# A four-layer graph network on one core: one-hots by VectorE, edge steps and the tail in another order

## The chip, the cores and the metric

The kernel runs on one core of one Trainium2 chip. The metric is the device time of one execution in microseconds. The kernel before takes 243.12 us in the median of three runs (242.83 to 243.68).

## The reference, cut to what matters

128 nodes with 512 features, 4096 edges sorted by target, four layers one after the other, each followed by a residual and a layer norm (LN). Everything is float32.

```
L0: q, k, v = x@Wq+bq, x@Wk+bk, x@Wv+bv            # 8 heads of 64
    scores masked by the adjacency, softmax over n, attn @ v, @ Wo + bo
    h1  = LN(x + attn_out)*g1 + be1                 # "LN1"
    out = LN(h1 + relu(h1@W1+b1)@W2 + b2)*g2 + be2  # "LN2"
x  = LN(x + out)
L1: h = mish([x[src], x[dst], edge_attr] @ W1 + b1) # 4096 edges
    m = mish(h @ W2 + b2);  agg = segment_sum(m, dst)
    u = mish([x, agg] @ W3 + b3);  y = x + u@W4 + b4
    out = LN(y)*gamma + beta
x  = LN(x + out)
L2: two graph convolutions, out = Ahat@relu(Ahat@(x@W1)+b1)@W2 + b2
x  = LN(x + out)
L3: h = x@Ws^T + (Cn@x)@Wn^T + bias;  out = LN(h)*gamma + beta
x  = LN(x + out)
```

x[src] @ W1a is computed as a matmul of A = x@W1a (128 nodes) with a one-hot matrix ST (node by edge) that picks the source of each edge; DT does the same for the targets. The edge_attr part of the product, 64 features deep, is computed ahead of time and kept in C.

## The kernel before, in words

Each engine has its own instruction list, in an order written out by hand, with semaphores between them; nothing is reordered at run time. The names:

- **Edge groups.** The 4096 edges are eight groups of 512, and four pairs of groups. ST and DT hold eight stretches of 512 columns, one for each group, in float32r. C holds 8 x 4 tiles of 128x512 (four blocks of 128 hidden features).
- **One-hots of the targets** (L523 to L530, and `onehot_out`, L319): TensorE turns Dbf, the bfloat16 one-hot with edges on the partitions, by 32 matmuls against an identity, in eight PSUM fillings over four banks. ScalarE copies each into DT (eight copies of 128x512, L321). This lies behind the product with Wo and ahead of the transposes of LN1's output.
- **One-hots of the sources** (`source_onehots`, L1015): the ids, spread by DMA to all partitions as two 1 MB pieces `ids0` and `ids1`, are compared with the partition's number by VectorE, eight instructions of 128x512, four ahead of the graph matrices (L1023) and four behind them.
- **Edge steps** (`edge_term`, L538). A step makes two C tiles: six matmuls (three terms, two groups) into two banks, which ScalarE reads with the bias added (`edge_term_out`, L323). Steps 0 to 11 (the ring) go over banks 5, 6, 7, 0 in turn; steps 12 to 15 over banks 1 to 4, around and behind the products A and B. A bank must have been read before it is filled again. Steps 0 to 2 lie between the four parts of the first feed-forward product (F1), steps 3 to 6 in the second (F2), steps 7 to 10 in the wait for LN2, step 11 behind the transposes of LN2's output xs (L661 to L665).
- **LN2 on VectorE.** `residual` (L888) takes each half of F2's result as it is signalled (f2_done), adds xw, takes statistics; then norm with gain, a second norm, xs. TensorE transposes xs into banks 3 and 4; VectorE makes xhi, xlo and xT, and TensorE computes A and B ("AB", L668 to L673).
- **Edge loop** (L753 on). For g = 0..7: `second_layer(g)` is 48 matmuls of 512 columns (h and W2, each split in a high and a low part), `first_layer(g+1)` 16, `sum_messages(g-1)` 8. VectorE and ScalarE work beside it: z1_out, z2_out, mish, low parts.
- **Tail.** update (W3), o = u@W4 (banks 2 and 4), residual with xw, norm with gain, y; the transposes of y; z = y@G1; r0; Ahat@r0; r1g; p1g; `p1g@G2` added to xw in banks 5 and 6; statistics; xs; the last layer in banks 4 and 0; last norms; output. GpSimd computes each 1/sqrt(var) (`inverse_root`, L284, tile rstd). WsR and WnR are transposed on the way (`turn`, eight of four transposes; ScalarE's `turned_out`, L434) and split in high (`ws_high`, L429) and low parts (`weight_low`, L1093).
- **SyncE's DMA list**, in order: inputs and weights up to W1raw; a wait for the last target one-hot and for the edge counts (L240, L241), F2; a wait for Wo's product, ids0, ids1; three rows of LN2; W2raw; a wait for xs, seven late rows, L1_b2; G1, G2; W3, W4, WsR, WnR each behind a group of the loop.

A source one-hot and a step of the ring:

```
v.tensor_scalar(ST_by_tile[:, q, h], row_ids[h][:, q], iota_col[:, 0:1], None, ALU.is_equal)
for i, (w, x) in enumerate([(Wchi, EAThi), (Wclo, EAThi), (Wchi, EATlo)]):
    for o in range(2):
        done = mm(banks[o][:, :], w[part, P * j:P * (j + 1)], x[part, q, :], start=i == 0, stop=i == 2)
```

Of the kernel before, what the change touches and what calls it, by code (L numbers as in the profile page):

```python
# [40 lines left out]
def gnn_kernel(nc, a, out):  # L41

    ctx = ExitStack()
    with ctx:
# [69 lines left out]
        thin = overlay(("bvo", 87, 2, F32), ("bvo_parts", 89, 2, F32R))  # L114
        ctx.enter_context(nc.sbuf_tensor("region", [P, 95 * D], F32))
# [19 lines left out]
        ST_by_tile = ST.rearrange("p (q o i s e) -> p q s i o e", q=PAIRS, o=2, i=GT, s=2)  # L135
# [22 lines left out]
        PRE = (bank[5], bank[6], bank[7], bank[0])  # L158
        EA_BANKS = (bank[4], bank[4], bank[3], bank[3])
        F1_BANKS = bank[1:5]  # L160
        DT_BANKS = (bank[7], bank[1], bank[2], bank[0])
# [20 lines left out]
        DT_UNIT, C_UNIT = 0, G  # L182
        RING_STEPS = KC * (PAIRS - 1)
        UNITS = C_UNIT + 2 * RING_STEPS
        TURNED_FIRST = 5
        LATE_BANKS = ((bank[3], bank[4]), (bank[1], bank[2]))

        S = {}
        for name in ("x_in warm_ready ids_in row_ids_in0 row_ids_in1 st_ready vecs_in ea_in wq_in0 wq_in1 wq_in2 wq_in3 wk_in0 wk_in1 wk_in2 wk_in3 ids_twice wv_in wo_in f1_in f2_in w1_in wc_in w2_in w3_in w4_in g_in ws_in wn_in b1g_in "
# [32 lines left out]
        def _(sp):  # L222
# [17 lines left out]
            sp.wait_ge(S["pre_done"], C_UNIT)  # L240
# [5 lines left out]
            for name in EARLY_ROWS[2:]:  # L246
                load_row(name)
            sp.dma_start(W2raw, w_view(a["L1_gnn_W2"])).then_inc(S["w2_in"], 16)


            sp.wait_ge(S["nx_ready"], 4)
            for name in LATE_ROWS:
                load_row(name)
            sp.wait_ge(S["pre_done"], C_UNIT + 2 * KC)
            load_row("L1_gnn_b2")
            sp.wait_ge(S["ab_done"], 2)
            sp.dma_start(G1, w_view(a["L2_gnn_W1"])).then_inc(S["g_in"], 16)
            sp.dma_start(G2, a["L2_gnn_W2"]).then_inc(S["g_in"], 16)
# [7 lines left out]
            sp.dma_start(WnR, w_view(a["L3_gnn_W_neigh"])).then_inc(S["wn_in"], 16)  # L266
            sp.wait_ge(S["y_final0"], 1)
# [24 lines left out]
        def _(act):  # L292
# [20 lines left out]
            for j in range(KC):  # L313
                bias_out(qT[:, j, :], quarter(bank[2], j), "L0_gnn_bq", j).then_inc(S["qk_ready"], 1)
            for j in range(KC):
# [3 lines left out]
            def onehot_out(dst, unit, g):  # L319
                act.wait_ge(S["pre_done"], unit + g + 1)  # L320
                act.activation(dst[:, GE * g:GE * (g + 1)], DT_BANKS[g % 4][:, :], ACT.Copy).then_inc(S["pre_read"], 1)  # L321

            def edge_term_out(steps):  # L323

                for s in steps:
                    q, j = s // KC, s % KC
                    for o in range(2):
                        k = 2 * s + o
                        if s < RING_STEPS:
                            act.wait_ge(S["pre_done"], C_UNIT + k + 1)  # L330
                            src, signal = PRE[(C_UNIT + k) % 4], "pre_read"
                        else:
                            act.wait_ge(S["late_done"], k - 2 * RING_STEPS + 1)
                            src, signal = LATE_BANKS[s % 2][o], "late_read"
                        bias_out(C[:, 2 * q + o, j, :], src[:, :], "L1_gnn_b1", j).then_inc(S[signal], 1)
# [24 lines left out]
            act.wait_ge(S["wc_in"], 32)  # L360
            act.activation(Wchi, Wc, ACT.Copy).then_inc(S["wc_hi"], 1)
            features_high(0)
            for g in range(G):
                onehot_out(DT, DT_UNIT, g)
            features_high(1)
            features_high(2)
            act.wait_ge(S["ao_done"], 1)
            act.wait_ge(S["wo_done"], 2)
            act.wait_ge(S["w1_in"], 16)
            for i in range(4):  # L370
                relu_out(i)
                w1_high(i)
                if i >= 1:
                    edge_term_out(range(i - 1, i))
            features_high(3)
            edge_term_out(range(3, RING_STEPS))
            act.wait_ge(S["w2_in"], 16)
            act.wait_ge(S["st_ready"], 2 * PAIRS)
# [59 lines left out]
            turned_out(range(TURNED_FIRST))  # L438
            for h in range(2):
                act.wait_ge(S["y2T_done"], h + 1)  # L440
                act.activation(half(flat(xT[:, :, :]), h), (bank[2], bank[4])[h][:, 0:D // 2], ACT.Copy).then_inc(S["y2T_ready"], 1)
            ws_high(0)
            ws_high(1)
            turned_out(range(TURNED_FIRST, 2 * KC))
            act.wait_ge(S["g1_done"], 1)
            act.activation(r1g, bank[3][:, 0:HID2], ACT.Relu).then_inc(S["g1_ready"], 1)
            ws_high(2)
            act.wait_ge(S["g2_done"], 1)
            act.activation(p1g, bank[4][:, 0:N], ACT.Copy).then_inc(S["g2_ready"], 1)
            ws_high(3)  # L450
# [19 lines left out]
        def _(pe):  # L470
# [44 lines left out]
            def free_bank(n):  # L515
                if n >= 4:
                    pe.wait_ge(S["pre_read"], n - 3)
                return PRE[n % 4]

            def turn_onehots(by_edge, groups):  # L520

                for g in groups:
                    b = DT_BANKS[g % 4]  # L523
                    if g >= 4:
                        pe.wait_ge(S["pre_read"], g - 3)
                    for i in range(GT):
                        done = mm(quarter(b, i), by_edge[:, tile_of(g, i), :], ident_bf[:, :], start=True, stop=True)
                    done.then_inc(S["pre_done"], 1)

# [7 lines left out]
            def edge_term(steps):  # L537

                for s in steps:
# [3 lines left out]
                    if s < RING_STEPS:  # L543
                        banks, signal = [free_bank(C_UNIT + 2 * s + o) for o in range(2)], "pre_done"
                    else:
                        if s >= RING_STEPS + 2:
                            pe.wait_ge(S["late_read"], 2 * (s - RING_STEPS - 1))
                        banks, signal = LATE_BANKS[s % 2], "late_done"
# [74 lines left out]
            pe.wait_ge(S["ident_bf_ready"], 1)  # L623
            pe.wait_ge(S["cols_ready"], 1)
            turn_onehots(Dbf, range(G))
            pe.wait_ge(S["ea_lo"], 1)
            turn_features(1)
            transpose_halves(O_BANKS, y, S["nx_ready"], 0, S["nT_done"])
            turn_features(2)
            pe.wait_ge(S["nT_ready"], 2)  # L630
            pe.wait_ge(S["f1_in"], 16)
            for i in range(4):
                if i < 2:
                    pe.wait_ge(S["pre_read"], 6 + i)
# [3 lines left out]
                if i == 1:  # L638
                    pe.wait_ge(S["wc_lo"], 1)
                if i >= 1:  # L640
                    edge_term(range(i - 1, i))
# [37 lines left out]
            def first_layer(g, js=range(KC), ks=range(len(terms))):  # L679

                for j in js:
# [3 lines left out]
                    elif ks[0] == 0:  # L685
                        pe.wait_ge(S["pre_read"], UNITS - 3 + u)
# [43 lines left out]
            pe.wait_ge(S["st_ready"], 2 * PAIRS)  # L730
# [46 lines left out]
            o_banks = (bank[2], bank[4])  # L777
            pe.wait_ge(S["u_hi"], 2)
            for b in range(2):
                columns_by(o_banks, uThi, W4hi, b, (0, 1), 0, None)  # L780
# [32 lines left out]
            pe.wait_ge(S["b1g_in"], 16)  # L813
            mm(bank[3][:, 0:HID2], ident[:, :], b1g[:, :], start=True, stop=False)
            pe.wait_ge(S["r0_ready"], 1)
            mm(bank[3][:, 0:HID2], Ahat[:, :], r0, start=False, stop=True).then_inc(S["g1_done"], 1)
            pe.wait_ge(S["wt_ready"], 2 * KC)
            pe.wait_ge(S["g1_ready"], 1)
            mm(bank[4][:, 0:N], r1g, Ahat[:, :], start=True, stop=True).then_inc(S["g2_done"], 1)
            for h in range(2):  # L820
                pe.wait_ge(S["xw_ready"], 1 + h)
                mm((bank[5], bank[6])[h][:, 0:D // 2], ident[:, :], half(xw, h), start=True, stop=False)
# [3 lines left out]

            pe.wait_ge(row_in["L3_gnn_bias"], 16)
# [35 lines left out]
        def _(dve):  # L863
# [24 lines left out]
            def residual(banks, extra, signal):  # L888

                for h in range(2):  # L890
                    dve.wait_ge(signal, h + 1)
# [77 lines left out]

            dve.wait_ge(S["scores_done"], 1)  # L970
# [22 lines left out]
            dve.wait_ge(S["wc_hi"], 1)  # L993
            v.tensor_tensor(Wclo, Wc, Wchi.bitcast(F32), ALU.subtract).then_inc(S["wc_lo"], 1)
# [20 lines left out]
            def source_onehots(h):  # L1015

                dve.wait_ge(S[f"row_ids_in{h}"], 16)
                for q in range(PAIRS):
                    v.tensor_scalar(ST_by_tile[:, q, h], row_ids[h][:, q], iota_col[:, 0:1], None, ALU.is_equal).then_inc(S["st_ready"], 1)

            source_onehots(0)
# [3 lines left out]
            source_onehots(1)  # L1025
# [5 lines left out]
            st = residual((bank[1], bank[2]), xw, S["f2_done"])  # L1031
# [8 lines left out]
            out_halves(xT_flat, xs_banks, S["nT_done"], 2, S["nT_ready"])  # L1040
            def w2_low(cs):
# [4 lines left out]
            dve.wait_ge(S["ab_done"], 1)  # L1046
            v.tensor_copy(Ahi, bank[1][:, :]).then_inc(S["ab_ready"], 1)
# [46 lines left out]

            for j in range(KC):
# [9 lines left out]
            for g in range(G):  # L1105
# [22 lines left out]
                z2_out(g, 3)  # L1128
                if g >= G - 2:
# [85 lines left out]
```

## Time and profile before

| | us |
|---|---|
| median of three runs | 243.12 (242.83 to 243.68) |
| the profiled execution | 242.47 |
| its span in the profile | 240.7 |
| PE (TensorE matmul) busy | 228.5 |
| DVE (VectorE) busy | 162.7 |
| ACT (ScalarE) busy | 130.1 |
| POOL (GpSimd) busy | 5.9 |

All times below are microseconds from the start of the span, except where a duration is meant. The span is 1.8 us less than the profiled execution's own time, and that execution is 0.65 us under the median. "PE" is TensorE, "L552" is a line of the kernel; a line can be that of a helper. The chain of waits is the work that ended last, followed back from the end.

### The profile page before, as it was taken

The numbers are of one execution on the slowest core, as the hardware profiler recorded it, in microseconds if no ns is written. First come the engines' busy times: TensorE is split into PE (matmuls) and PEld (weight loads), VectorE is DVE, ScalarE is ACT, GpSimd is POOL, SyncE is SP. The second block draws the span as 40 slices with busy tenths as digits, with TensorE's granted clock in tenths as the row PEclk, the third lists the DMA queues.
The fourth block names the chain that finished last, engine by engine and source line by source line (L and its number), as shares of the span: only waits on it lengthen the run. The fifth ranks groups of instructions, "written<-read, shape, count | busy, mean of one in ns | idle before, by whom it ended". The sixth has DMA issues, their size and how long they took to land.

```text
span 240.7 us, 3320 instructions
## 1 busy us (share of the span) xinstructions
PE 228.5 (95%) x1255; PEld 184.3 (77%) x1255; DVE 162.7 (68%) x291; ACT 130.1 (54%) x240; POOL 5.9 (2%) x17
## 2 busy tenths in 40 slices
PE   8999999997999999999999999999999999998980
PEld 4958788664766887888888888888888888997670
DVE  3956846687679655865856847758568556567695
ACT  0635289748549835745635646557475533159500
POOL 1000100001000000000000000000000000000101
PEclk9999999999999999999999999999999999999996
DMA  6999979910680000009031040040000000000001
GB/s 228 309 407 404 389 235 408 342 54 0 190 242 7 0 0 0 3 18 326 5 106 72 0 176 0 3 174 0 0 0 3 0 0 0 3 0 1 3 0 44
DMA packets 12039, 24.97 MB, mean 104 GB/s; under 512 B 988, under 2 KB 1908, under 8 KB 11640
## 3 DMA queue, kind: packets, MB, share of 16 engines
q1 hardware_dynamic: 11232, 24.25, 28.2%
q10 hardware_dynamic: 792, 0.51, 0.8%
q8 instruction: 10, 0.16, 0.3%
q14 instruction: 5, 0.04, 0.1%
HBM read 24.50 MB, written 0.26 MB: 103 GB/s over the span
## 4 chain that ended last, share of the span: by engine, by line
PE 89%; DVE 4%; ACT 3%; issue 2%; POOL 1%; POOLq 0%; DVEq 0%; ACTq 0%
PE bank L706 36%; PE bank L689 13%; PE bank L495 8%; PE bank L504 6%; PE bank L552 4%; PE bank L569 3%; PE bank L716 3%; PE bank L717 3%; PE bank L593 2%; PE bank L513 1%; PE bank L484 1%; ACT DT L321 1%; ACT WsT L434 1%; PE bank L668 1%; POOL rstd L284 1%
## 5 line engine op out<-in xcount | busy, mean ns | idle before, releaser
L706 PE MATMUL bank<-W2hi,Hhi 128*128 128x512 f32 x128 | 49.8, 389 | 0.0
L706 PE MATMUL bank<-W2hi,Clo 128*128 128x512 f32 x128 | 49.8, 389 | 0.0
L706 PE MATMUL bank<-W2lo,Hhi 128*128 128x512 f32 x128 | 49.8, 389 | 0.0
L394 ACT ACTIVATE Mhi<-M 128x512 fp32r<-128x512 f32 x32 | 20.2, 632 | 44.4 <-DVE M L1075 44.4
L1080 DVE TENSOR_TENSOR Mlo<-M,Mhi 128x512 fp32r<-128x512 f32 x32 | 22.1, 690 | 22.0 <-ACT M L395 22.0
L1075 DVE TENSOR_TENSOR M<-bank,b2r 128x512 f32<-128x512 f32 x32 | 22.0, 688 | 12.6 <-PE bank L717 7.6
L706 PEld LDWEIGHTS bank<-W2hi,Clo 128*128 128x128 f32 x128 | 24.0, 188 | 5.0
L706 PEld LDWEIGHTS bank<-W2lo,Hhi 128*128 128x128 f32 x128 | 24.0, 188 | 5.0
L706 PEld LDWEIGHTS bank<-W2hi,Hhi 128*128 128x128 f32 x128 | 24.0, 188 | 5.0
L387 ACT ACTIVATE Hhi<-C 128x512 fp32r<-128x512 f32 x32 | 20.0, 624 | 11.4 <-DVE C L1061 11.1
L305 ACT ACTIVATE C<-bank,cols 128x512 f32<-128x512 f32 x32 | 19.9, 686 | 10.5 <-PE bank L552 10.5
L1061 DVE TENSOR_TENSOR C<-bank,C 128x512 f32<-128x512 f32 x32 | 21.4, 689 | 5.1 <-PE bank L689 4.1
L1066 DVE TENSOR_TENSOR Clo<-C,Hhi 128x512 fp32r<-128x512 f32 x32 | 22.0, 688 | 3.7 <-ACT C L388 3.6
L689 PE MATMUL bank<-ST,AB 128*128 128x512 f32 x64 | 20.0, 399 | 0.0
L388 ACT ACTIVATE C<-C 128x512 f32<-128x512 f32 x32 | 19.7, 617 | 0.0
L395 ACT ACTIVATE M<-M 128x512 f32<-128x512 f32 x32 | 19.7, 616 | 0.0
L689 PE MATMUL bank<-DT,AB 128*128 128x512 f32 x64 | 19.4, 390 | 0.0
L689 PEld LDWEIGHTS bank<-ST,AB 128*128 128x128 f32 x64 | 11.6, 188 | 3.9 <-DVE C L1061 1.0
L689 PEld LDWEIGHTS bank<-DT,AB 128*128 128x128 f32 x64 | 12.0, 188 | 2.6
L716 PE MATMUL bank<-Mhi,Dg 128*128 128x512 f32 x32 | 12.6, 395 | 0.0
L717 PE MATMUL bank<-Mlo,Dg 128*128 128x512 f32 x32 | 12.5, 389 | 0.0
L284 POOL TENSOR_TENSOR rstd<-mv,mhalf 128x1 f32<-128x1 f32 x8 | 4.7, 588 | 206.1 <-DVE mv L915 193.8
(227 smaller groups left out, 332.7 us busy)
## 6 DMA issues: line engine op xcount, KB each, us to landing
F<-in_L_gnn_W SPq DMA_DIRECT2D x2, 2048.0 KB, 14.1
W1raw<-in_L_gnn_W SPq DMA_DIRECT2D x1, 2048.0 KB, 22.7
ids<-in_src SPq DMA_DIRECT2D x2, 1024.0 KB, 13.0
W<-in_L_gnn_W SPq DMA_DIRECT2D x1, 2048.0 KB, 9.2
Wq<-in_L_gnn_Wq SPq DMA_DIRECT2D x4, 256.0 KB, 3.7
Wk<-in_L_gnn_Wk SPq DMA_DIRECT2D x4, 256.0 KB, 5.6
Wv<-in_L_gnn_Wv SPq DMA_DIRECT2D x1, 1024.0 KB, 9.2
ea<-in_edge_attr SPq DMA_DIRECT2D x1, 1024.0 KB, 11.2
```

Of the source, the lines that this page charges most:

```text
L305: return act.activation(dst, src, func, bias=cols[:, col[name] + j:col[name] + j + 1])
L387: act.activation(Hhi[:, g % 2, j, :], C[:, g, j, :], ACT.Mish)
L388: act.activation(C[:, g, j, :], C[:, g, j, :], ACT.Mish).then_inc(S["h_hi"], 1)
L394: act.activation(Mhi[:, t, :], M[:, t, :], ACT.Mish)
L689: done = mm(ST1[u % 3][:, :], w[:, P * j:P * (j + 1)], x[:, GE * g:GE * (g + 1)], start=k == 0, stop=k == len(terms) - 1)
L706: done = mm(ST2[t][:, :], x[:, c, e], w[:, c, :], start=c == 0 and i == 0, stop=c == KC - 1 and i == 2)
L716: mm(AGG[:, :], Dg[:, t, :], Mhi[:, t, :], start=g == 0 and t == 0, stop=False)
L717: done = mm(AGG[:, :], Dg[:, t, :], Mlo[:, t, :], start=False, stop=g == G - 1 and t == GT - 1)
L1061: v.tensor_tensor(C[:, g, j, :], ST1[u % 3][:, :], C[:, g, j, :], ALU.add).then_inc(S["z1_read"], 1)
L1066: v.tensor_tensor(Hlo[:, g, j, :], C[:, g, j, :], Hhi[:, g % 2, j, :].bitcast(F32), ALU.subtract).then_inc(S["h_lo"], 1)
L1075: v.tensor_tensor(M[:, t, :], ST2[t][:, :], row["L1_gnn_b2"], ALU.add).then_inc(S["z2_read"], 1)
L1080: v.tensor_tensor(Mlo[:, t, :], M[:, t, :], Mhi[:, t, :].bitcast(F32), ALU.subtract).then_inc(S["m_lo"], 1)
```

## The change

- **Target one-hots** are no longer turned by TensorE or copied by ScalarE; VectorE makes them as it makes those of the sources. For pairs 0 and 1 (groups 0 to 3) both kinds are made ahead of the loop, in four instructions each of 128x512: sources for both halves ahead of the graph matrices; targets of half 0 inside LN2's residual, between its two halves; targets of half 1 behind the copy into xT. For groups 4 to 7 each group takes one instruction of 512 and two of 256 columns, in the loop at g = 1 to 4, behind z2_out(g, 2) and z2_out(g, 3).
- **DMAs.** The target ids are loaded twice, 1 MB for each half: into ids0 and ids1 as soon as the source one-hots have read these, then into two pieces for the loop; the source ids once more for the loop (2 MB). W2raw is now queued behind the first target ids, and the wait for the target one-hots ahead of F2 is gone. Late rows, G1 and G2 are loaded at the end of the loop instead of behind LN2.
- **Edge steps.** Steps 0, 1, 2 go where the target one-hots were turned, step 3 behind the third part of F1, steps 4 and 5 into F2, steps 6 to 10 behind F2 (five in LN2), step 11 as before. Step 1 uses banks 1 and 2, step 8 banks 3 and 4, the others (5, 6) or (7, 0): three pairs in LN2. The transposes of xs wait until step 8 has been read.
- **Wchi and Wclo** are made earlier (ScalarE between the biases of q and k, VectorE ahead of the softmax).
- **Tail.** Half 1 of the residual xw is put into bank 4 by a matmul with the identity ahead of u@W4, so VectorE takes half 1's statistics from the bank. The row L2_b2 is put into banks 5 and 6 by TensorE ahead of time; xw is then (y - mean) * rstd alone, and r0 is finished before it. Low parts of WsT are moved away from in front of r0 and from beside GpSimd's root (`weight_low` 0, 1 and 2). ScalarE copies four turned blocks, not five, ahead of the transposed y.

```diff
-            sp.wait_ge(S["pre_done"], C_UNIT)
             sp.wait_ge(S["ct_done"], 1)
             sp.dma_start(F2, w_view(a["L0_gnn_W2"])).then_inc(S["f2_in"], 16)
...
+            for h in range(2):
+                sp.wait_ge(S["st_ready"], 2 * (h + 1))
+                sp.dma_start(other[f"ids{h}"], by_partition(a["dst"][E // 2 * h:E // 2 * (h + 1)], E // 2)).then_inc(S[f"dst_ids_in{h}"], 16)
             sp.dma_start(W2raw, w_view(a["L1_gnn_W2"])).then_inc(S["w2_in"], 16)
...
-            turn_onehots(Dbf, range(G))
-            pe.wait_ge(S["ea_lo"], 1)
+            edge_term(range(0, 1))
             turn_features(1)
+            edge_term(range(1, 2))
+            turn_features(2)
             transpose_halves(O_BANKS, y, S["nx_ready"], 0, S["nT_done"])
-            turn_features(2)
+            edge_term(range(2, 3))
...
-                if i == 1:
-                    pe.wait_ge(S["wc_lo"], 1)
-                if i >= 1:
-                    edge_term(range(i - 1, i))
+                if i == 2:
+                    edge_term(range(3, 4))
...
                 columns_by((bank[1], bank[2]), ffT, F2, h, range(0, 3), 0, FC - 1)
-                edge_term(range(2 * h + 3, 2 * h + 4))
+                edge_term(range(h + 4, h + 5))
                 columns_by((bank[1], bank[2]), ffT, F2, h, range(3, FC - 2), 0, FC - 1)
-                edge_term(range(2 * h + 4, 2 * h + 5))
...
-            edge_term(range(7, RING_STEPS - 1))
+            edge_term(range(6, 8))
             pe.wait_ge(S["graph_ready"], 2)
+            pe.wait_ge(S["ea_lo"], PAIRS)
+            edge_term(range(8, RING_STEPS - 1))
+            pe.wait_ge(S["pre_read"], 18)
             transpose_halves((bank[3], bank[4]), xs, S["nx_ready"], 2, S["nT_done"])
...
+            for h in range(2):
+                first_onehots(ST_by_tile, "row_ids_in", h)
             dve.wait_ge(S["graphT_done"], 1)
...
-            st = residual((bank[1], bank[2]), xw, S["f2_done"])
+            st = residual((bank[1], bank[2]), xw, S["f2_done"], lambda: first_onehots(DT_by_tile, "dst_ids_in", 0))
...
+                if 1 <= g < G - 3:
+                    loop_sources(g + 3)
...
+            pe.wait_ge(S["xw_ready"], 1)
+            mm(o_banks[1][:, 0:D // 2], ident[:, :], half(xw, 1), start=True, stop=False)
...
-            weight_low(WsTlo, WsT, WsThi, (0,), "ws")
...
-            chain(off_mean(0))
             dve.wait_ge(S["rstd_ready"], norms[0])
             v.tensor_scalar(r0, r0, rstd[:, 0:1], -1.0, ALU.mult, ALU.mult).then_inc(S["r0_ready"], 1)
...
-            weight_low(WsTlo, WsT, WsThi, (2,), "ws")
             dve.wait_ge(S["stat_ready"], norms[0])
```

## Rows read from the trace of the kernel before

**Rows 1.** The page: busy time of an engine; the chain of waits by engine.

```profile
PE 228.5 (95%) x1255; PEld 184.3 (77%) x1255; DVE 162.7 (68%) x291; ACT 130.1 (54%) x240; POOL 5.9 (2%) x17
PE 89%; DVE 4%; ACT 3%; issue 2%; POOL 1%; POOLq 0%; DVEq 0%; ACTq 0%
```

**Rows 2.** The chain of waits, 28 to 33 us: start, duration, what.

```profile
28.06 0.24 PE bank L527 x4
28.32 2.07 ACT DT L321 x4
...
30.84 0.44 PE bank L534 x4
```

**Rows 3.** The chain of waits through both feed-forward products, 32 to 55 us.

```profile
32.35 3.84 PE bank L504 x32
...
41.94 0.90 PE bank L552 x6
...
53.87 1.07 PE bank L495 x4
```

**Rows 4.** VectorE in order of time, 45 to 65 us: start, duration, line.

```profile
45.84 2.45 DVE L1019 TENSOR_SCALAR ST<-ids,iota_col 128x512 fp32r<-128x512 int32 x4
49.33 0.35 DVE L1023 TENSOR_SCALAR Ahat<-bank,small 128x128 f32<-128x128 f32 x1 [1.04 <-PE bank L656]
...
52.12 0.71 DVE L1028 TENSOR_TENSOR xw<-y,rows 128x512 f32<-128x512 f32 x1
...
54.05 0.43 DVE L893 BATCH_NORM_STATS2 stats<-y 128x6 f32<-128x256 f32 x1
55.03 0.42 DVE L892 TENSOR_TENSOR y<-bank,xw 128x256 f32<-128x256 f32 x1 [0.55 <-PE bank L495]
...
64.54 0.69 DVE L1047 CAST AB<-bank 128x512 fp32r<-128x512 f32 x1 [2.02 <-PE bank L673]
```

**Rows 5.** The chain of waits: the transposes of xs.

```profile
59.98 0.67 PE bank L484 x4
```

**Rows 6.** DMA issues: size, median us from issue to landing.

```profile
WsR<-in_L_gnn_W_self SPq DMA_DIRECT2D x1, 1024.0 KB, 5.3
ids<-in_src SPq DMA_DIRECT2D x2, 1024.0 KB, 13.0
```

**Rows 7.** By stretch: busy PE, PEld, DVE, ACT, POOL; PE clock granted; DMA share, GB/s.

```profile
31.00:32.00 1.00, 1.00 (x11) 0.92 (x9) 0.46 (x2) 1.00 (x3) 0.00 (x0) 1.00 0.09 33
...
56.00:60.00 4.00, 2.46 (x19) 1.22 (x15) 3.20 (x7) 4.00 (x8) 1.10 (x2) 1.00 0.00 0
236.00:240.00 4.00, 0.00 (x0) 0.00 (x0) 1.76 (x5) 0.51 (x1) 0.55 (x1) 0.57 0.20 66
```

**Rows 8.** ScalarE in order of time: edge steps read while VectorE works on LN2.

```profile
55.85 4.80 ACT L305 ACTIVATE C<-bank,cols 128x512 f32<-128x512 f32 x8 [0.69 <-PE bank L552]
```

**Rows 9.** VectorE in the loop: group 5 without, group 6 with an added instruction.

```profile
171.85 0.69 DVE L1080 TENSOR_TENSOR Mlo<-M,Mhi 128x512 fp32r<-128x512 f32 x1 [1.22 <-ACT M L395]
...
186.87 0.68 DVE L1093 TENSOR_TENSOR W4lo<-W,W4hi 128x512 fp32r<-128x512 f32 x1
188.17 0.69 DVE L1080 TENSOR_TENSOR Mlo<-M,Mhi 128x512 fp32r<-128x512 f32 x1 [0.62 <-ACT M L395]
```

**Rows 10.** The chain of waits near the start (two identity matmuls) and in the tail.

```profile
4.62 0.86 PE bank L490 x4
...
210.55 2.88 PE bank L495 x24
...
216.86 0.49 ACT WnT L434
...
219.70 0.37 DVE xs L1157
...
224.45 0.87 POOL rstd L284
```

**Rows 11.** GpSimd in order of time: the root before it in the tail.

```profile
217.84 0.55 POOL L284 TENSOR_TENSOR rstd<-mv,mhalf 128x1 f32<-128x1 f32 x1 [2.15 <-DVE mv L1148]
```

More of the change, by code:

```diff
@@ L359, in _ @@
             act.preload_act_table_set("mish")
-            act.wait_ge(S["wc_in"], 32)
-            act.activation(Wchi, Wc, ACT.Copy).then_inc(S["wc_hi"], 1)
             features_high(0)
-            for g in range(G):
-                onehot_out(DT, DT_UNIT, g)
+            edge_term_out(range(0, 1))
             features_high(1)
+            edge_term_out(range(1, 2))
             features_high(2)
+            edge_term_out(range(2, 3))
             act.wait_ge(S["ao_done"], 1)
@@ L513, in keep_warm @@
                     mm(b[:, :], warm[:, :], warm[:, :].unsqueeze(1).to_broadcast([P, 4, P]), start=True, stop=True)
[L515 to L528, printed above, removed]
             def turn_features(q):
@@ L542, in edge_term @@
                         pe.wait_ge(S["ea_lo"], q + 1)
[L543 to L548, printed above, removed]
+                    banks, signal = step_banks(s), "pre_done" if s < RING_STEPS else "late_done"
+                    if 2 <= s < RING_STEPS and s != 8:
+                        pe.wait_ge(S["pre_read"], 2 * made_earlier(s))
+                    elif s >= RING_STEPS + 2:
+                        pe.wait_ge(S["late_read"], 2 * (s - RING_STEPS - 1))
                     for i, (w, x) in enumerate([(Wchi, EAThi), (Wclo, EAThi), (Wchi, EATlo)]):
@@ L820, in _ @@
             for h in range(2):
-                pe.wait_ge(S["xw_ready"], 1 + h)
-                mm((bank[5], bank[6])[h][:, 0:D // 2], ident[:, :], half(xw, h), start=True, stop=False)
+                pe.wait_ge(S["xw_ready"], 2 + h)
+                mm((bank[5], bank[6])[h][:, 0:D // 2], ident[:, :], half(xw, h), start=False, stop=False)
             pe.wait_ge(S["g2_ready"], 1)
@@ L886, in bank_statistics, with residual @@
                 return stats.rearrange("p h s -> p (h s)")
-            def residual(banks, extra, signal):
+            def residual(banks, extra, signal, between=None):
                 for h in range(2):
+                    if h == 1 and between:
+                        between()
                     dve.wait_ge(signal, h + 1)
@@ L968, in features_low @@
                 v.tensor_tensor(EATlo[:, q, :], EA_BANKS[q][:, :], EAThi[:, q, :].bitcast(F32), ALU.subtract).then_inc(S["ea_lo"], 1)
+            dve.wait_ge(S["wc_hi"], 1)
+            v.tensor_tensor(Wclo, Wc, Wchi.bitcast(F32), ALU.subtract).then_inc(S["wc_lo"], 1)
             dve.wait_ge(S["scores_done"], 1)
@@ L1013, in _, with first_onehots @@
             features_low(3)
[L1015 to L1021, printed above, removed]
+            def first_onehots(by_tile, arrived, h):
+                dve.wait_ge(S[f"{arrived}{h}"], 16)
+                for q in range(2):
+                    v.tensor_scalar(by_tile[:, q, h], row_ids[h][:, q], iota_col[:, 0:1], None, ALU.is_equal).then_inc(S["st_ready"], 1)
+            for h in range(2):
+                first_onehots(ST_by_tile, "row_ids_in", h)
             dve.wait_ge(S["graphT_done"], 1)
@@ L1128, in _ @@
                 z2_out(g, 3)
+                if 1 <= g < G - 3:
+                    loop_targets(g + 3)
                 if g >= G - 2:
@@ L1143, in _ @@
                 v.tensor_tensor(half(flat(uTlo), h), half(flat(uT), h), half(flat(uThi), h).bitcast(F32), ALU.subtract).then_inc(S["u_lo"], 1)
-            st = residual((bank[2], bank[4]), xw, S["o_done"])
-            norm_gain(y[:, :], y[:, :], r("L1_gnn_gamma"), xb_late, S["y2_ready"], st)
+            dve.wait_ge(S["xw_ready"], 1)
+            dve.wait_ge(S["o_done"], 1)
+            chain(v.tensor_tensor(half(y, 0), bank[2][:, 0:D // 2], half(xw, 0), ALU.add))
+            chain(v.bn_stats(stats[:, 0, :], half(y, 0)))
+            dve.wait_ge(S["o_done"], 2)
+            chain(v.bn_stats(stats[:, 1, :], bank[4][:, 0:D // 2]))
+            norm_gain((y, bank[4]), y[:, :], r("L1_gnn_gamma"), xb_late, S["y2_ready"], stats.rearrange("p h s -> p (h s)"))
             dve.wait_ge(S["y2_ready"], 2)
@@ L1153, in _ @@
             chain(v.scalar_tensor_tensor(out=r0, in0=G1sum, scalar=mv[:, 0:1], in1=bank[7][:, 0:HID2], op0=ALU.mult, op1=ALU.subtract))
-            r("L2_gnn_b2")
-            def off_mean(h):
-                return v.tensor_scalar(half(xs, h), half(y, h), mv[:, 0:1], None, ALU.subtract)
-            chain(off_mean(0))
             dve.wait_ge(S["rstd_ready"], norms[0])
             v.tensor_scalar(r0, r0, rstd[:, 0:1], -1.0, ALU.mult, ALU.mult).then_inc(S["r0_ready"], 1)
-            for h in range(2):
-                if h == 1:
-                    chain(off_mean(1))
-                v.scalar_tensor_tensor(out=half(xw, h), in0=half(xs, h), scalar=rstd[:, 0:1], in1=half(row["L2_gnn_b2"], h),
-                                       op0=ALU.mult, op1=ALU.add).then_inc(S["xw_ready"], 1)
-            weight_low(WsTlo, WsT, WsThi, (1,), "ws")
+            halves(lambda d, x, h: v.tensor_scalar(d, x, mv[:, 0:1], rstd[:, 0:1], ALU.subtract, ALU.mult), xw[:, :], y[:, :], S["xw_ready"])
+            weight_low(WsTlo, WsT, WsThi, (0, 1), "ws")
             st = bank_statistics((bank[5], bank[6]), S["g3_done"])
```

104 lines of the change are left out of this document (67 added, 37 removed).

## The prediction

> **What bounds the kernel now.** I read the page first. TensorE is busy 228.5 us of a span of 240.7, and the chain of waits is 89% PE [rows 1]. So work taken off TensorE shows in full, except where TensorE waits for a chain on another engine. Next I read the chain of waits in order of time, to find these places. Three matter. At LN1 TensorE turns target one-hots while VectorE normalizes; there the chain runs through ScalarE's one-hot copies, so the one-hots are the bound and not the norm [rows 2]. From 32.35 to 54.94 all pieces are TensorE's, with an edge step of 0.90 us seven times among them [rows 3]. At LN2 VectorE is the bound: half 1 of the residual starts at 55.03, as soon as F2 is done [rows 4], and the transposes of xs follow at 59.98 [rows 5]. The loop is TensorE alone. The tail is short waits passed between engines [rows 10].
>
> **One-hots out, steps 0 to 2 in (LN1).** From Wo's end at 28.06 to F1's start at 32.35 pass 4.29 us. After the change TensorE does there: step 0, features, step 1, features, the four transposes of y (0.45, as four such for the features), step 2. That is 3 x 0.90 + 2 x 0.44 + 0.45 = 4.03 [rows 2, 3]. The transposes begin at 28.06 + 2 x 1.34 = 30.74 instead of 30.84 + 0.44 = 31.28, so VectorE's copies into xT end half a microsecond earlier too, under step 2. Gain 0.26; I take 0.25. ScalarE loses eight copies (2.07 for four) and gets six step outputs at 0.60 [rows 2, 8]: hidden. Wchi and Wclo move to idle stretches ahead of the scores: 0.
>
> **F1 and F2.** Seven steps of 0.90 lie between 32.35 and 54.94 before, three (3, 4, 5) after: 4 x 0.90 = 3.6. F2 would end at 54.94 - 0.25 - 3.6 = 51.1. Its weights no longer wait for the last one-hot (30.84) to be asked for, and the stretch in which the DMA engines lie almost idle (0.09 at 31 to 32) fills up [rows 7]; so neither F2 nor the source ids should be late.
>
> **LN2: what is late next.** This is where I part from 3.85 us. VectorE's list now has the target one-hots of half 0 ahead of the residual's half 1, and these wait for a DMA that can be issued only when the source one-hots of half 0 have read the same buffer. When is that? The last part of F1 ends one step and the 0.25 earlier, at 40.8 instead of 41.94 [rows 3]; and ScalarE then has no step output (1.2) ahead of the last features. The first shift alone gives 1.15, both give 2.3; but VectorE's low parts of W1 run to 43.7, and that of the last features behind them to 44.25. So the source one-hots start at 44.25 instead of 45.84. Two of four instructions (2.45 for four) end at 45.5 [rows 4], and the DMA is issued at 45.6. A lone 1 MB load takes 5.3 us to land; 1 MB behind a full queue took 13.0 [rows 6]. W2raw is queued behind this load now, and what is ahead of it (F2, ids, three rows) starts as soon as W1raw is through instead of 1.7 us later, so I place it by the lone row and take 5.4. Landing 51.0; two one-hots 1.3; half 1 begins at 52.3. VectorE's own work ahead of it (the other two one-hots to 46.7, the graph matrices 0.6, and what runs from 52.12 to 54.48 now, 2.4) ends at 49.7 and doesn't bind [rows 4]. Half 1 moves from 55.03 to 52.3: **gain 2.7** of 3.9, the DMA takes 1.2.
>
> A page speaks to this price: the Trainium skill, "DMA: Bandwidth & Descriptors", section "Anatomy of one DMA", gives about 2.0 us plus the bytes over 436 GB/s, fitted on another queue. By it the load would be an estimated 4.4 us and the time 1.0 us shorter, 238.8. The row of this trace has 5.3 [rows 6], which decides.
>
> **TensorE and ScalarE in LN2.** Steps 6 to 10 start at 51.1. ScalarE needs 4.80 us for eight tiles, 1.2 a step [rows 8]. It reads step 6 by 53.0, 7 by 54.2, 8 by 55.4, 9 by 56.6. Steps 9 and 10 reuse the banks of 6 and 7, so TensorE ends step 10 at about 55.6. The transposes of xs come 4.95 us behind half 1 [rows 4, 5], at 57.25, when step 8 has long been read; step 11 needs step 9, read as well. So the fifth step is free, and TensorE idles about 1.6 us. Even with no DMA wait (transposes at 56.1) all of it just fits. The target one-hots of half 1 (1.3) lie behind xT, in VectorE's wait for A, which was 2.0 us [rows 4]: 0, if their load is there by 59.8; it is issued at 46.8, so it has 13 us. W2raw is queued behind it and has until about 60.
>
> **Loop.** VectorE gets 0.6 + about 0.7 us in each of g = 1 to 4. VectorE waits there for ScalarE, 1.22 us; in group 6 an instruction of 0.68 stands in the same place now, and the wait is 0.62 [rows 9]: it takes the waiting time and nothing else. Cost 0; without that cover 4 x 1.3 = 5.2 at most. The new 4 MB of ids land while DMA is nearly idle; the late rows have 45 us. Nothing waits on them: 0.
>
> **Tail.** (a) The identity matmul of xw's half 1 costs 0.43 (0.86 for two), in front of a chain that is TensorE's [rows 10]; in return one add of 0.42 and its hand-over leave VectorE's line. The gain's multiplication comes in two halves now, some 0.1 longer than one of 512. Together 0 to -0.1. (b) The copy of the fifth turned block (0.49) no longer stands in front of the transposed y: 0.3, as then the transposes bind [rows 10]. (c) r0 no longer waits for the subtraction (0.37), but TensorE has turns, b1g and the new b2 (0.43) in front of Ahat@r0, so of 0.7 that r0 is early only (b)'s shift survives. (d) GpSimd's root took 0.87 beside a VectorE instruction (L1093, low part of WsT), 0.55 without one [rows 10, 11]: that instruction is moved away, 0.3. The last products stay TensorE's. Sum (a) to (d): -0.05 + 0.3 + 0 + 0.3, near **0.6**; bounds -0.1 (the two matmuls fully exposed, root gained) and 1.1.
>
> **Sum.** 2.7 + 0.6 = 3.3. The profiled execution, 242.47 for a span of 240.7, would come to 239.2 and a span of 237.4. It lies 0.65 under the median of the runs, which the forecast is for: 243.12 - 3.3 = **239.8**.
>
> **Rivals.**
> - *The target ids don't hold LN2 up* (they land by 49.8, or the source one-hots are earlier than I have them). Then F2 is the bound: 3.9 + 0.6 = 4.5, 238.6. For it: 44.25 is built from several shifts, each good to some 0.2, and a landing time from one row can be off by 1 either way. Against: 5.3 for a lone load. Chance 0.2.
> - *The target ids land late*, behind the ids, rows and with the second 1 MB and W2raw pressing: every us past 5.4 goes into LN2 one for one, with F2's result lying ready and the whole rest of the kernel behind it. The total gain is 8.7 less the landing time. It turns at 8.7 us; by the row of 13.0 the kernel would be 4.3 slower, 247.4. Against: by my count 4.75 MB are queued from 30.6 on, done about 44, before this load is issued. Chance of slower by over 0.3%: 0.04; that it lands 1 to 3 us later than I say, 239.8 to 242: 0.12.
> - *The tail gives nothing* or a little back, its matmuls on a chain that TensorE already fills: 240.4 to 240.6. Chance 0.12.
> - *TensorE's clock falls in LN2.* The granted clock was 1.00 from 56 to 60 with TensorE busy 2.46 of 4 us, and fell to a mean of 0.57 at 236 to 240, with nothing on it [rows 7]. In the new LN2 it has 2.4 of the last 4 us ahead of the transposes; so it should stay at 2.4 GHz. If it fell to 1.2, AB (24 matmuls, 5.7 us) would take up to 5.7 more: 245.5. Chance 0.02.
>
> **How the numbers follow.** My case has 0.5. The range goes from the first rival's 238.6, with a little for the tail, to the late landing's 242: 238.5 to 241.8. What a measurement of this kernel can tell from no change is about 0.3%, 0.7 us. Faster by more than that: all of my case, the first and the third rival, most of the moderate delay, 0.90. Same 0.05, slower 0.05.
>
> **What would show it.** Right: no one-hot matmuls at LN1, F1 starting near 32.1; F2 ending near 51.1; VectorE idle about 1.2 us ahead of its first target one-hot, released by a DMA and starting near 51; xs transposes near 57.2; AB's start 2.7 us earlier (58.8 for 61.55); the stretch from AB to the end of the loop as long as before; root of layer L2 0.55 long. Wrong: target one-hot without a wait (then 238.6), or a wait of 3 us and more; waits of TensorE for z1_read, z2_read or m_lo in groups 1 to 5; an AB stage longer than 5.7 us.

## The result, and the profile after

The changed kernel takes 240.57 us in the median of four runs (239.57 to 241.22), the kernel before beside it 243.17 (242.83 to 243.68): ratio 0.9886, 95% interval 0.9863 to 0.9909. The forecast was 239.8, between 238.5 and 241.8. The profiled execution took 239.57 for a span of 237.8, 2.9 less than before's 240.7.

The page of the changed kernel, for [rows 1]:

```profile
PE 226.3 (95%) x1229; PEld 183.6 (77%) x1229; DVE 167.1 (70%) x301; ACT 126.1 (53%) x232; POOL 5.5 (2%) x17
PE 87%; DMA 4%; ACT 3%; SPq 2%; issue 2%; DVE 1%; POOL 0%; POOLq 0%; DVEq 0%; ACTq 0%
```

The 4% of DMA are the load of Wv, at the start. Wo's product ended at 28.74 instead of 28.06, so this profile carries 0.68 us that I don't count to the change (in a second profile of the same kernel the product ended at 28.28). The delay begins before anything that was changed: the first product with Wq starts at 5.84 instead of 5.41, and Wv then lands 9.9 us after its issue instead of 9.2. All later readings are best taken as distances.

The chain of waits of the changed kernel, LN1 to the first weights of AB, for [rows 2, 3, 5]:

```profile
28.74 0.88 PE bank L560 x4
29.62 0.59 PE bank L543 x4
30.22 0.89 PE bank L560 x6
31.11 0.59 PE bank L543 x4
31.69 0.44 PE bank L508 x4
32.13 0.89 PE bank L560 x3
33.02 5.56 PE bank L528 x48
38.58 0.90 PE bank L560 x6
...
51.20 0.94 PE bank L560 x6
52.14 5.31 ACT C L329 x9
57.45 0.13 issue
57.58 0.67 PE bank L508 x4
```

No one-hot matmul is left. F1 starts 4.28 us behind Wo's product (before: 4.29), F2 ends at 51.20, 18.2 us after F1's start (before: 22.6), and the transposes of xs (L508) start at 57.58 instead of 59.98. One line misleads: the chain puts the 5.3 us ahead of the transposes down to ScalarE's reads. TensorE waits there for two things, step 8 read and xs, and VectorE in order of time, for [rows 4], shows the one that came last:

```profile
44.91 2.41 DVE L1039 TENSOR_SCALAR ST<-ids,iota_col 128x512 fp32r<-128x512 int32 x4
...
49.59 0.43 DVE L913 BATCH_NORM_STATS2 stats<-y 128x6 f32<-128x256 f32 x1
51.42 1.31 DVE L1039 TENSOR_SCALAR DT<-ids,iota_col 128x512 fp32r<-128x512 int32 x2 [1.41 <-DMA ids<-in_dst]
52.65 0.41 DVE L912 TENSOR_TENSOR y<-bank,xw 128x256 f32<-128x256 f32 x1
...
57.02 0.73 DVE L930 TENSOR_SCALAR xs<-y,mv,rstd 128x256 f32<-128x256 f32 x2 [0.66 <-POOL rstd L308]
```

VectorE has half 0 of the residual done at 50.0, waits 1.41 us for the DMA of the target ids, makes two one-hots and starts half 1 at 52.65, 1.4 after F2's end. From half 1 to the transposes pass 4.93 us, as before (4.95). In the second profile of this kernel (experiment 1) the chain itself runs through this DMA.

In the loop VectorE, for [rows 9], first group with a source one-hot and two target one-hots:

```profile
102.89 0.76 DVE L1120 TENSOR_SCALAR ST<-src_ids,iota_col 128x512 fp32r<-128x512 int32 x1
104.20 0.69 DVE L1103 TENSOR_TENSOR Mlo<-M,Mhi 128x512 fp32r<-128x512 f32 x1 [0.55 <-ACT M L417]
104.81 0.68 DVE L1098 TENSOR_TENSOR M<-bank,b2r 128x512 f32<-128x512 f32 x1
105.41 0.82 DVE L1125 TENSOR_SCALAR DT<-dst_ids,iota_col 128x256 fp32r<-128x256 int32 x2
106.71 0.69 DVE L1103 TENSOR_TENSOR Mlo<-M,Mhi 128x512 fp32r<-128x512 f32 x1 [0.48 <-ACT M L417]
```

The waits for ScalarE shrink from 1.22 to 0.55 and 0.48, and nothing moves. From AB's start to the transposes of agg in the tail pass 143.8 us in both kernels.

The tail of the changed kernel in the chain of waits, and GpSimd's roots, for [rows 10, 11]:

```profile
202.99 0.44 PE bank L508 x4
...
208.05 0.43 PE bank L790 x2
208.49 2.87 PE bank L519 x24
...
215.52 1.13 PE bank L822 x8
...
218.18 0.22 PE bank L832 x2
218.40 0.43 PE bank L834 x2
...
221.87 0.56 POOL rstd L308
```

```profile
215.52 0.55 POOL L308 TENSOR_TENSOR rstd<-mv,mhalf 128x1 f32<-128x1 f32 x1 [2.28 <-DVE mv L1190]
221.87 0.55 POOL L308 TENSOR_TENSOR rstd<-mv,mhalf 128x1 f32<-128x1 f32 x1 [5.81 <-DVE mv L1201]
```

From the transposes of agg to ScalarE's last instruction pass 31.88 us (202.99 to 234.87) against 32.39 before (205.37 to 237.76): the tail gives 0.51, of which 0.32 is the root (0.55 instead of 0.87).

### The profile page after: what moved, and what is told of

It reads as the page before. It is cut to its first block, busy times and chain, and to the rows that moved or that the text cites. A ratio compares the mean times of both kernels' runs of the same rounds, so it can differ in the third digit from the quotient of the medians.

```text
span 237.8 us, 3276 instructions
## 1 busy us (share of the span) xinstructions
PE 226.3 (95%) x1229; PEld 183.6 (77%) x1229; DVE 167.1 (70%) x301; ACT 126.1 (53%) x232; POOL 5.5 (2%) x17
## 4 chain that ended last, share of the span: by engine, by line
PE 87%; DMA 4%; ACT 3%; SPq 2%; issue 2%; DVE 1%; POOL 0%; POOLq 0%; DVEq 0%; ACTq 0%
PE bank L717 37%; PE bank L700 13%; PE bank L519 8%; PE bank L528 6%; PE bank L560 5%; DMA Wv<-in_L_gnn_Wv 4%; PE bank L727 3%; PE bank L728 3%; ACT C L329 2%; PE bank L601 2%; PE bank L738 1%; PE bank L508 1%; PE bank L677 1%; PE bank L589 1%; SPq L244 1%
```

## The experiments

**1. The changed kernel again,** unchanged, to see how far its executions differ.

> The changed kernel once more, to see how far its executions differ. Theory: its runs spread from 239.6 to 241.2 with granted clocks of 0.992 to 0.984, and the 0.7 us that the first 28 us lost in the profiled run (Wv landed late) is scatter of the first loads and no effect of the change: ratio 0.987 to 0.991 again, and in this profile the product with Wo ends anywhere between 28.0 and 29. Rival: the 0.7 us belong to the change (Wchi between the biases of q and k), then they are there again in every profile of it.

Median 240.33 of six (238.83 to 241.85), ratio 0.988 [0.984, 0.992]. With the four of the result these are ten executions of the changed kernel, here with their mean granted clocks:

```
us      238.83 238.88 239.49 239.57 | 240.24 240.90 241.16 241.22 241.37 241.85
clock     .993   .993   .991   .992 |   .987   .984   .985   .984   .988   .986
```

Two kinds: four with a clock of 0.991 and more, mean 239.2, and six with 0.988 and less, mean 241.1. The sixteen executions of the kernel before, run beside them, lie within 242.6 to 243.7 with clocks of 0.989 to 0.994. The first loads do scatter: Wo's product ended at 28.28 in this profile, and between 28.4 and 29.2 in those of experiments 2 to 11. All of these lie behind the 28.06 of the kernel before, which has a single profile, 0.65 us under its median; so a small share of the change in this delay isn't ruled out. The two kinds have another cause than the first loads, as experiment 5 shows.

**2. Target one-hots of half 0 behind xT.**

```diff
-            st = residual((bank[1], bank[2]), xw, S["f2_done"], lambda: first_onehots(DT_by_tile, "dst_ids_in", 0))
+            st = residual((bank[1], bank[2]), xw, S["f2_done"])
...
-            first_onehots(DT_by_tile, "dst_ids_in", 1)
+            for h in range(2):
+                first_onehots(DT_by_tile, "dst_ids_in", h)
```

> Both halves of the target one-hots behind xT instead of half 0 inside the residual. Theory (LN2 waits for the DMA of the target ids): half 1 of the residual starts when F2 is done, the transposes of xs come 1.3 to 1.4 us earlier against the end of F2, and the kernel is 0.8 to 1.4 us faster than the changed one (240.6), less what the four one-hots (2.5 us) behind xT delay A's high part, about 0.4. Rival (LN2 is bound by ScalarE's reads of steps 8 and 9, so the wait is hidden anyway): no change within 0.3.

Median 238.31 (237.76 to 238.50), ratio 0.9796 [0.9777, 0.9815]: 2.3 below the changed kernel's median, and 0.9 below its four fast-clock executions. VectorE of this kernel:

```profile
51.41 0.42 DVE L912 TENSOR_TENSOR y<-bank,xw 128x256 f32<-128x256 f32 x1 [1.29 <-PE bank L519]
...
58.80 2.54 DVE L1039 TENSOR_SCALAR DT<-ids,iota_col 128x512 fp32r<-128x512 int32 x4
61.44 0.69 DVE L1071 CAST AB<-bank 128x512 fp32r<-128x512 f32 x1
```

Half 1 follows F2's end (51.32) at once. The transposes of xs came at 56.36, 1.3 earlier against F2's end. All four clocks were 0.992 to 0.995. The target ids were what ended LN2's wait; the rival, ScalarE's reads, is out. This version is faster than both kernels. Of the 2.3 us only the 0.9 are the wait for the ids; the rest is that none of its four executions is of the slower kind.

**3. W2raw ahead of the target ids.**

```diff
             for h in range(2):
                 sp.wait_ge(S["st_ready"], 2 * (h + 1))
+                if h == 0:
+                    sp.dma_start(W2raw, w_view(a["L1_gnn_W2"])).then_inc(S["w2_in"], 16)
                 sp.dma_start(other[f"ids{h}"], by_partition(a["dst"][...
-            sp.dma_start(W2raw, w_view(a["L1_gnn_W2"])).then_inc(S["w2_in"], 16)
```

> W2raw (1 MB) is queued between the wait for the source one-hots and the first target ids, so these land later. Theory: 1 MB at some 390 GB/s is 2.6 us; the ids land after 7.7 us instead of 5.1, VectorE's wait grows from 1.4 to about 4.0, and the whole kernel is 2.4 to 2.7 us slower than the changed one, about equal to the kernel before. Rival (the wait has slack behind it): less than 1 us slower.

Median 244.47 (243.26 to 245.12), ratio 1.005 [1.0035, 1.0065]: 3.9 slower than the changed kernel, more than the load can explain. VectorE's wait is as forecast, but by stretch (busy PE, PEld, DVE, ACT, POOL; clock granted; DMA) the profile shows a second thing:

```profile
54.58 1.27 DVE L1040 TENSOR_SCALAR DT<-ids,iota_col 128x512 fp32r<-128x512 int32 x2 [4.10 <-DMA ids<-in_dst]
```

```profile
56.00:60.00 4.00, 0.02 (x2) 0.00 (x0) 3.27 (x7) 2.48 (x5) 0.98 (x2) 0.78 0.22 86
60.00:62.00 2.00, 1.29 (x6) 0.99 (x8) 1.33 (x4) 0.00 (x0) 0.11 (x1) 0.50 0.20 37
62.00:64.00 2.00, 2.00 (x8) 1.16 (x9) 2.00 (x6) 0.59 (x2) 0.00 (x0) 0.50 0.89 336
64.00:66.00 2.00, 2.00 (x8) 1.62 (x7) 0.76 (x2) 2.00 (x3) 0.00 (x0) 0.73 0.38 152
```

TensorE does nothing from 56.0 to 60.7, and its granted clock goes to 0.50, 1.2 GHz, until into the AB products.

**4. Step 6 back into F2.**

```diff
                 columns_by((bank[1], bank[2]), ffT, F2, h, range(3, FC - 2), 0, FC - 1)
+                if h == 1:
+                    edge_term(range(6, 7))
...
-            edge_term(range(6, 8))
+            edge_term(range(7, 8))
```

> Step 6 goes back from LN2 into the second half of F2, so four steps are left in LN2. Theory (the target ids end LN2's wait, F2 has 1.4 us to spare): F2 ends 0.9 to 1.1 us later, the residual's half 1 starts when it did, no change within 0.3. Rival (TensorE's work ahead of LN2 is the bound, and the fifth step in LN2 is where the gain comes from): 0.9 us slower.

Median 239.35 of six. Four have clocks of 0.992 to 0.994 and lie at 238.91, 239.04, 239.09 and 239.61, mean 239.2, the same as the changed kernel's; two have 0.985 and 0.987, at 241.27 and 241.50. So a step more or less in LN2 changes nothing as long as the ids are the last to come: within one kind the expectation held. (By the medians it did not, 239.35 against 240.33 and 240.57, since here two of six are of the slower kind and there six of ten.) The profile taken is of the second kind and shows the place:

```profile
54.00:58.00 4.00, 2.13 (x18) 1.14 (x14) 3.17 (x6) 4.00 (x8) 1.10 (x2) 1.00 0.85 321
58.00:60.00 2.00, 2.00 (x10) 1.04 (x8) 1.76 (x6) 0.37 (x1) 0.00 (x0) 0.53 0.54 134
60.00:62.00 2.00, 2.00 (x7) 1.54 (x6) 1.59 (x4) 1.76 (x3) 0.00 (x0) 0.61 0.96 393
62.00:64.00 2.00, 2.00 (x10) 1.61 (x9) 0.15 (x1) 1.31 (x1) 0.00 (x0) 1.00 0.01 4
```

TensorE is idle for about 1.9 us ahead of xs, and step 11 and the first AB products run at half clock. The profiled changed kernel had about the same idle stretch (2.0 us, and 1.8 in the profile of experiment 1) and stayed at 1.00. Note that the stretch is here with four steps in LN2, as many as before the change.

**5. TensorE kept busy in LN2.** `keep_warm(6, bank[3])` is six matmuls of 512 columns on constants, whose results nobody reads. It fills the idle stretch and changes nothing else.

```diff
             pe.wait_ge(S["pre_read"], 18)
+            keep_warm(6, bank[3])
             transpose_halves((bank[3], bank[4]), xs, S["nx_ready"], 2, S["nT_done"])
```

> The changed kernel with six matmuls of 512 columns on constants (1.36 us, results unused) in bank 3 ahead of the transposes of xs, where TensorE idles for 2 us. Theory (its two kinds of execution, about 239 with a mean granted clock of 0.991 to 0.993 and 241 to 242 with 0.984 to 0.988, differ in whether TensorE's clock falls to 1.2 GHz behind this idle stretch): all executions lie between 238.7 and 239.8, none has a clock under 0.990, and the median is 1.0 to 1.5 us below that of the changed kernel. Rival (the spread comes from the first loads or from elsewhere): runs at 241 and more stay.

Median 239.39 of five (238.35 to 239.77), clocks 0.990 to 0.996, ratio 0.9826 [0.9801, 0.9851]: no execution above 239.8, and the median 0.9 to 1.2 below the changed kernel's. The matmuls themselves cost nothing in this place:

```profile
56.09 1.47 PE L537 MATMUL bank<-warm 128*128 128x512 bf16 x6 [0.20 <-ACT C L329]
57.39 0.60 PE L508 MATMUL bank<-ident,xs 128*128 128x128 f32 x4
```

The fallen clock is the cause of the second kind of execution: with six of ten in that kind, five of five outside it would come by chance about once in a hundred times.

**6. The late ids and the clock taken apart:** experiment 3 with 18 such matmuls.

```diff
             pe.wait_ge(S["pre_read"], 18)
+            keep_warm(18, bank[3])
```

> The kernel with W2raw ahead of the target ids (244.5, its profile at 1.2 GHz behind LN2), with 18 matmuls on constants (4.1 us) in TensorE's idle stretch of LN2. Theory (its 5.4 us over the undisturbed executions of the changed kernel, 239.1, are 2.5 of late ids and 2.9 of the fallen clock): clock 1.00 behind LN2, 241.4 to 242.0. Rival (the late ids alone explain it): still 244.

Median 242.28 (241.93 to 242.77), clocks 0.993 to 0.996. Against experiment 3 the clock is worth 2.2 us, against experiment 5 the late ids 2.9: they land 7.6 us after their issue instead of 4.6 to 5.1 (the profiles of the changed kernel and of experiments 1, 4 and 5), and the issue itself is 0.4 us later, behind that of W2raw. Both terms are there; I had put the first at 2.9 and the second at 2.5, so the median is 0.3 above my bracket. In its profile the clock reads 1.00 where experiment 3 had 0.50:

```profile
56.00:60.00 4.00, 3.97 (x18) 1.68 (x18) 3.28 (x7) 2.28 (x4) 0.98 (x2) 1.00 0.22 84
60.00:62.00 2.00, 1.47 (x11) 0.89 (x10) 1.64 (x5) 0.00 (x0) 0.12 (x1) 1.00 0.18 33
```

**7. TensorE's work at LN1 put back,** as 13 matmuls without use, on the kernel of experiment 2.

```diff
             pe.wait_ge(S["wc_lo"], 1)
+            keep_warm(13, bank[7])
             edge_term(range(0, 1))
```

> On the kernel with both target one-hots behind xT (238.3): 13 matmuls of 512 columns on constants (13 x 0.227 = 2.95 us, as much as the removed 32 target one-hots took) ahead of step 0 behind Wo's product. Theory (TensorE's work at LN1 shows in full, since the norm and the later waits have no more than 0.3 us to spare): 2.6 to 3.0 us slower, 241.1. Rival (LN1's own chain on VectorE and GpSimd, 28.9 to 31.4, covers it): at most 1.5 slower.

Median 241.28 (240.86 to 241.41), 2.97 above experiment 2. In the traces the 13 matmuls take 2.81 us, and from Wo's product to the transposes of xs pass 2.80 more. Work on TensorE at LN1 shows to the full: the norm's own chain covers none of it.

**8. Low part 2 beside the root,** on the kernel of experiment 2.

```diff
             v.bn_aggr(mv[:, :], st).then_inc(S["stat_ready"], 1)
+            weight_low(WsTlo, WsT, WsThi, (2,), "ws")
             dve.wait_ge(S["stat_ready"], norms[0])
...
-            weight_low(WsTlo, WsT, WsThi, (2,), "ws")
             dve.wait_ge(S["nm_hi"], 1)
```

> On the kernel with both target one-hots behind xT (238.3): the low part 2 of WsT goes back beside GpSimd's root in L2's norm. Theory: the root takes 0.87 instead of 0.55 again, 0.3 us slower. Rival (the root's length has nothing to do with what VectorE does beside it): 0.55 and no change.

The root is long again, and the one behind it is not:

```profile
220.36 0.86 POOL L308 TENSOR_TENSOR rstd<-mv,mhalf 128x1 f32<-128x1 f32 x1 [5.81 <-DVE mv L1202]
230.36 0.55 POOL L308 TENSOR_TENSOR rstd<-mv,mhalf 128x1 f32<-128x1 f32 x1 [9.13 <-DVE mv L935]
```

Median 238.53 (238.07 to 238.67), 0.2 above experiment 2: the direction is right, but the executions of both scatter by 0.6 to 0.7, so the time alone doesn't show it; the instruction's length does. The Trainium skill, "SBUF — State Buffer", section "Who interferes with whom", says that a VectorE instruction with two SBUF inputs contends with a GpSimd instruction that reads SBUF; the low part is such an instruction. The trace agrees: 0.86 us beside it, 0.55 without.

**9. The matmul for xw undone,** on the kernel of experiment 2: `residual` and `norm_gain` on one source as before, no identity matmul ahead of u@W4.

> On the kernel with both target one-hots behind xT (238.3): the identity matmul of xw's half 1 and the norm over two sources are undone, half 1 is added by VectorE again. Theory (TensorE's 0.43 in front of u@W4 and VectorE's saving cancel): within 0.2 us. Rival (the matmul gains): 0.4 slower; rival (it costs): 0.4 faster.

Median 238.40 (237.95 to 238.76) against 238.31: nothing, as expected. TensorE's 0.43 and VectorE's saving cancel, to 0.1 us in the traces (z starts 12.42 behind the transposes of agg here, 12.53 in experiment 2).

**10. The whole old tail,** on the kernel of experiment 2: TensorE's, ScalarE's and VectorE's lists from agg to the last layer as in the kernel before.

> On the kernel with both target one-hots behind xT (238.3): the whole tail as in the kernel before (xw, r0, rows, turned blocks, low parts, root). Theory (of the changed kernel's gain the tail brought 0.5 us: 0.3 the root, 0.2 the shorter wait for y transposed, nothing xw and r0): 238.8. Rival (the tail's parts give nothing together): 238.3; rival (the forecast's 0.6 and more): 239.0 and more.

Median 238.58 (238.37 to 238.73), 0.27 above experiment 2, in the medians half of what the traces show. By the chain, transposes of agg to ScalarE's last instruction take 32.39 us here (201.55 to 233.94) and 31.87 in experiment 2 (201.80 to 233.67): 0.52. In their first loads the two profiled executions differ by 0.3 the other way (Wo's product ends at 28.54 and 28.83), so scatter of that size can account for the rest; 0.5 is the distance in the traces, and the medians resolve 0.3.

**11. Each one-hot of the loop made twice,** on the kernel of experiment 2.

```diff
                 dve.wait_ge(S["loop_src_in"], 16)
+                chain(v.tensor_scalar(ST_by_group[:, g], src_ids[:, g // 2, g % 2], iota_col[:, 0:1], None, ALU.is_equal))
...
                 for h in range(2):
+                    chain(v.tensor_scalar(DT_by_group[:, g, h], dst_ids[h][:, g // 2, g % 2], iota_col[:, 0:1], None, ALU.is_equal))
```

> On the kernel with both target one-hots behind xT (238.3): each one-hot made in the loop is made twice, 1.3 to 1.5 us more of VectorE in each of g = 1 to 4. Theory (VectorE waits there for ScalarE, 0.5 us are left of it, and TensorE asks for the low part only in the next group): TensorE stays without a gap, no change within 0.2. Rival (the loop's VectorE work is near its limit): 0.3 to 4 slower.

Median 237.91 (237.59 to 238.53): not slower. VectorE's waits for ScalarE are used up in these groups, and TensorE is still busy throughout (experiment 2 has 88.46 us of VectorE in the same stretch):

```profile
76.00:200.00 124.00, 124.00 (x556) 102.78 (x555) 93.83 (x152) 68.84 (x123) 0.00 (x0) 1.00 0.25 85
```

## Why the prediction was right, and where not

**The median** lies 0.8 above the forecast and inside the range. The path held step by step, but the number is good partly by luck: two misses of opposite sign. LN2 and the tail gave 3.6 us in the trace (3.8 in the profile of experiment 1), where I had 3.3, and the executions whose clock stays up come to 239.2, 4.0 under the kernel before. One rival that I had priced and all but dismissed (chance 0.02) takes 1.4 of that back.

**LN1: size off by 0.25.** I counted a turn of features at 0.44 us. That is its time behind the one-hots; behind an edge step it is 0.59, twice. F1 starts 4.28 behind Wo's product, not 4.03, so the gain of 0.25 was 0. The idea was right: experiment 7 shows that TensorE binds there.

**F1 and F2: 4.4 instead of 3.6.** A step costs 0.90 and also what it does to its neighbours. Without steps between, F1's first parts take 5.56 for three (before 3.84 for two and 1.98 for the third), the turn behind F1 0.44 instead of 0.58, and F2's later matmuls of a half (x10 in the chain) 2.36 instead of 1.49 + 1.06. That is 0.8 for four steps, which I had not counted.

**LN2: right in kind and size.** The source one-hots started at 44.91; my 44.25 plus this profile's late 0.68 is 44.93. That it fits so closely is luck: F1 started 0.25 later than I had it, and its parts took 0.26 less. The ids landed in 5.1 us, where I took 5.4; the estimate by the Trainium skill ("DMA: Bandwidth & Descriptors", section "Anatomy of one DMA") was 4.4, and the measurement stands nearer to the row of 5.3. VectorE waited 1.41, I had said 1.2. Against Wo's product the transposes of xs came 3.1 us earlier, I had 2.7 from there; the load that landed 0.3 sooner is most of it. Experiment 2 shows that this DMA was the last to come, experiment 4 that TensorE's fifth step was not, experiments 3 and 6 that later ids go into the time about one for one. The slower rival's sum was right too: it gives 8.7 less the landing time, 1.1 us of gain at 7.6, and experiment 6 has 1.0 (243.3 to 242.3). This too has two misses in it that cancel: there the ids are also asked for 0.4 later, and with the clock held up the change is worth more than the sum says.

**The clock: the step that failed.** I wrote that TensorE would have 2.4 of the last 4 us ahead of the transposes, as before, and so stay at 2.4 GHz. The profile has 1.88 of 4 (53.5 to 57.5), where before had 2.55 (55.9 to 59.9). One reason is the miss in F1 and F2: against Wo's product the steps of LN2 were done 0.7 sooner than I had them, xs only 0.35 sooner, so the idle stretch grew from my 1.6 to 2.0. And the prediction compares busy shares only, not how the idle time lies. TensorE's idle time in the changed kernel, then in the kernel before:

```profile
53.50:57.50 4.00, 1.88 (x12) 0.92 (x12) 3.16 (x8) 4.00 (x8) 1.09 (x2) 1.00 0.87 317
57.58 0.67 PE L508 MATMUL bank<-ident,xs 128*128 128x128 f32 x4 [2.01 <-ACT C L329]
```

```profile
57.27 0.51 PE L552 MATMUL bank<-EAThi,Wchi 64*128 64x512 f32 x2 [0.76 <-ACT C L305]
58.42 0.50 PE L552 MATMUL bank<-EAThi,Wchi 64*128 64x512 f32 x2 [0.18 <-ACT C L305]
59.98 0.67 PE L484 MATMUL bank<-ident,xs 128*128 128x128 f32 x4 [0.60 <-DVE xs L910]
```

Before, with two pairs of banks, TensorE waited between its steps until ScalarE had read a bank, and the idle time came in three short pieces. With the third pair the steps run back to back but for 0.2 us, and the idle time is one stretch of 2.0 us at the end. The fifth step is not the reason: experiment 4 has four steps, as before, and a stretch of 1.9. With such a stretch, six of ten executions are of the kind with the lower mean clock. The price is 1.9 us (239.2 to 241.1), not the 5.7 I gave as its most: in the profile of experiment 4 the clock is back before AB is half through. This moves the median by more than a microsecond; without it (experiment 5) the change is worth 4.1 us, more than my 3.3.

**Loop: 0, as said** (experiment 11: even twice the work is hidden). **Tail: 0.5 for 0.6.** The root gave 0.32 of 0.32; of the earlier y transposed came 0.15 (z 12.53 behind the transposes of agg, before 12.68) of 0.3; xw and r0 nothing, r0 since TensorE's own list ahead of Ahat@r0 (L822 to L832 in the chain) has no gap left.

What stays open: why one execution falls and the next does not with the same idle stretch. Whether it is the length of the stretch or the lower busy share ahead of it that matters isn't shown either, as no experiment changes one alone. Of the 4.0 us that the executions with the clock up gain, the traces show 3.6 to 3.8; the rest lies within the scatter of the first loads. The changed kernel's own low-clock executions were seen only by their mean clock; the place is shown by the profile of experiment 4 and by experiment 5.

## What to carry to other kernels

When TensorE's work is removed ahead of a norm, ask what VectorE's list holds at that point and which load it waits for; a buffer that must be read before its next content can be asked for is a chain of its own (read, issue, 5 us), and an operation that waits on it belongs behind the norm, not inside it. More banks let all available work run at the front of a wait and leave one long idle stretch at its end: compare the longest stretch and the busy share just before the next burst with those of the kernel before, and if the times of one kernel form two groups with two mean clocks, put harmless matmuls there before reasoning further. Here the median over both groups hides a third of what the change is worth.

## What the runs showed of the hardware that I had not expected

- With 1.8 to 2.0 us without a matmul ahead of xs, TensorE's clock fell to 1.2 GHz in some executions and not in others: in the profile of experiment 4 (1.87 us) it fell, in the two of the changed kernel (2.01 and 1.77 us) it did not. With 0.7 us (experiments 2 and 7 to 11, 25 executions) or with matmuls in the stretch (experiments 5 and 6, eleven) no mean clock is under 0.989. In experiment 3, with 4.7 us without a matmul, it was at 0.50 (and ten of its eleven executions have mean clocks of 0.977 to 0.981). The Trainium skill, "TensorE: Matmul & The Clock Gate", section "What's actually happening", says that the clock follows how busy the engine has been, and that the moments at which this is judged are not tied to the kernel's start. The trace agrees with the first (0.50 after idle time, 1.00 where matmuls filled it); the second would fit that equal executions end differently, but no run here shows it.
- A turn of features (four transposes of 128 columns) takes 0.44 us behind other matmuls of 128 columns and 0.59 behind an edge step; what follows a step (matmuls of 64 rows and 512 columns) takes 0.15 to 0.2 us longer than without it. The step's own 0.90 has such a share too: behind another step one takes 0.68 (their starts at 51.93 and 52.61 in the changed kernel).
